# Six shared PSUM banks, attention products of both row halves together, and maxima moved by small DMAs in a gated cross-attention block

## The chip, the cores and the metric

The kernel runs on one core of a Trainium2 chip. The core has a matmul engine (PE, its weight loads are shown as PEld), a vector engine (DVE), a scalar engine for activations (ACT), a general engine (POOL) and a sync engine (SP) that issues DMAs. Each engine works through its own list of instructions in order; semaphores are the only coupling. PE writes to PSUM, which has eight banks of 128 partitions by 512 fp32 numbers, and DVE and ACT read it. The metric is the time of one launch in microseconds (us), the median of some runs.

## What is computed

The reference, cut to what matters (8 batches, 100 queries of width 128, 1444 keys of width 64, 16 heads of width 64, fp32):

```
qh = layernorm(x) @ Wq ; kh = ctx @ Wk ; vh = ctx @ Wv      # split into 16 heads
attn = softmax(qh kh^T / 8)
x = x + tanh(g_xattn) * ((attn @ vh) @ Wo + bo)
z = fp4(layernorm(x))
h = silu(z @ fp4(w_gate)^T) * (z @ fp4(w_up)^T)
x = x + tanh(g_ffn) * (fp4(h) @ fp4(w_down)^T)
```

fp4() rounds blocks of 16 numbers to a grid of 8 magnitudes times a scale of the block.

## The kernel before

Wq is folded with Wk and Wv with Wo ahead of the loop, so that each head scores and sums the raw context of width 64. A **group** is one batch and half of the heads: 8 heads times 100 queries, 800 rows. There are 16 groups (g = 0 to 15), and an even and an odd one make a batch. The 1444 keys are cut into 12 chunks of 120 or 121.

A group has 24 **slots**, one for each chunk c and half k of the 800 rows. In a slot PE makes one tile of scores (keys on partitions, 400 rows as columns) with two matmuls into one bank: L914 (query times key, a split into high and low parts in the 128 partitions) and L915 (the low part of the query, and in seven further rows of `q_ls`, one for each tile of 116 rows, the negated row maximum, so that the bank holds score minus maximum). ACT turns the tile into `probs` (L749, exp). Later L931 multiplies chunks 2j and 2j+1 of one half with the context: two fp32 matmuls into the upper and lower 64 partitions of bank k of `attn`, called a **pair** here. In the profile a pair is four matmul records.

The row maximum is needed before the scores of a group. So while group g runs, PE also makes the scores of group g+1 with rows on partitions (L840, 7 tiles of 116 rows by 3 parts of 482 keys, 21 **maxima**, numbered 0 to 20), DVE reduces each (L1071, `max3`) and then folds them (`max_tiles`, L1112, into `maxes`, one column for each tile). The **shift** use transposes `maxes` with PE into a bank (L843), and DVE spreads it over the seven rows of `q_ls` (L1075).

PSUM is held as two banks of scores (slot modulo 2), two of `attn`, and a ring of four for everything else, handed out in the order of use: the folded query (`q`, L820, read by four ACT copies L638 into `q_hh`, two for each half of the rows, and by two DVE subtractions `split_q`, L1053), the 21 maxima, the shift, the softmax sums (L850), the output products `proj` (L857, read by ACT head by head, L661), and the feed-forward products of the other batches (`xT`, `zT`, `gate`, `up`, `hT`, `down`). A use waits until the use four before it has been read.

The order on every engine is written by hand, by tables of slot numbers: a use that stands at slot s in a table is issued after the scores of slot s, and the pairs of a slot come after its ring uses. `PV_SLOTS` places the 12 pairs (numbers from 24 on fall into the next group), `MAX_SLOTS` the maxima for even and odd groups, `POST_SLOTS` sums and `proj`, `COPY_SLOTS` ACT's copies of `attn`, `CTX_COPY_SLOTS` ACT's six copies that split the next batch's keys, `KLO_AT` the place on POOL of an accumulating DMA that completes those keys (`k_hl`, L600). The first maximum of a group waits for the first two of ACT's four query copies, and in an odd group also for that DMA. Groups 0 and 15 have tables of their own; that of group 15 sets most of its pairs two by two already.

Of the kernel before, what the change touches and what calls it, by code (L numbers as in the profile page):

```python
# [49 lines left out]
SCORE_BANKS, RING_BANKS = 2, 4  # L50
# [20 lines left out]
MAX_SLOTS = [{1: 2, 4: 1, 5: 1, 6: 1, 7: 4, 8: 1, 11: 2, 12: 2, 13: 2, 14: 1, 16: 2, 17: 2}, {1: 1, 3: 2, 6: 1, 7: 4, 8: 1, 9: 1, 10: 2, 13: 1, 14: 2, 15: 4, 17: 1, 18: 1}]  # L71
MAX_TILES_SLOT = [19, 18]
SHIFT_SLOT = [20, 20]
FFN_SLOTS = {1: ('zT', 0), 3: ('gate', 0), 4: ('up', 0)}
DOWN_SLOTS = {4: ('hT', 0), 6: ('hT', 1), 8: ('down', 0)}
LAST_FFN_SLOTS = {**FFN_SLOTS, 20: ('hT', 0), 21: ('hT', 1), 22: ('down', 0)}
W_SLOTS = {(2, 3): ('wT', 0), (2, 14): ('wT', 1), (2, 15): ('wT', 2), (2, 16): ('wT', 3), (2, 19): ('wT', 4), (2, 20): ('wT', 5)}
POST_SLOTS = [{7: ('sum', 0), 8: ('proj', 0), 9: ('proj', 1)}, {6: ('sum', 0), 8: ('proj', 0), 9: ('proj', 1)}]
XT_SLOT = 18
LN2_SLOTS = [13, 14]  # L80
LN2_APPLY_SLOT = 16
Z_SLOTS = [16, 18, 19, 19, 20, 21, 22, 22, 22]
SIGMOID_SLOTS = [4, 5]
H_SLOTS = [18, 19, 20, 21, 22, 22, 23, 23, 23]
# [6 lines left out]
Q_LO_SLOTS = [0, 0]  # L91
HEAD_SLOTS = [7, 7, 8, 9, 9, 9, 9, 9]
LN1_SLOTS = [2, 4, 12]
CTX_COPY_SLOTS = [7, 7, 11, 11, 12, 12]
KLO_AT = 7
# [10 lines left out]
FIRST_MAX_TILES_SLOT, FIRST_SHIFT_SLOT = 20, 21  # L106
# [3 lines left out]
POOL_AT = {'ln1': 2, 'ln2': 6, 'swiglu': (1, 2, 4), 'heads': 5}  # L110


def ring_keys(g, slot):
    keys = []
    pre = g + 1 < GROUPS
    maxima, shift_slot = (MAX_SLOTS[g % 2], SHIFT_SLOT[g % 2]) if g else (FIRST_MAX_SLOTS, FIRST_SHIFT_SLOT)
# [16 lines left out]
    if pre and slot == shift_slot:  # L133
        keys += [("shift", 0)]
# [10 lines left out]
def number_ring():  # L145
    index, n = {}, 0
    for key in START:
        index[(-1, key)] = n
        n += 1
    for g in range(GROUPS):  # L150
        for slot in range(SLOTS):
            for key in ring_keys(g, slot):
                index[(g, key)] = n
                n += 1
    for key in FINISH:
        index[(GROUPS, key)] = n
        n += 1
    return index


RING = number_ring()

# [26 lines left out]
class Turn:  # L189
# [20 lines left out]
    def ring(self, key):  # L210

        i = RING[(self.g, key)]
        return i % RING_BANKS, i // RING_BANKS + 1
# [10 lines left out]
def xattn_ffn(nc, x, ctx_in, g_xattn, g_ffn, Wo, bo, w_gate, w_up, w_down, ctxT_in, WqT, WkT, WvT, out):  # L224
    with ExitStack() as es:
# [7 lines left out]
        scores = es.enter_context(nc.psum_tensor("scores", [128, SCORE_BANKS, 512], F32))  # L233
# [39 lines left out]
        maxes = sb("maxes", [128, TILES])  # L273
# [56 lines left out]
        max_done = sem("max_done")  # L330
        scores_full = sem("scores_full")
# [121 lines left out]
        def _(sp):  # L453
# [36 lines left out]
            def group(t):  # L490
# [15 lines left out]
                if t.g % 2 == 0 and t.g >= 4 or t.g == GROUPS - 1:  # L506
                    store(t)
# [751 lines left out]
```

## Time and profile before

| | |
|---|---|
| median of 3 runs | 548.21 us (547.03 to 548.56) |
| the profiled execution | 547.66 us, of which the span of the trace is 545.8 us |
| PE, PEld busy | 532.4 us (98%), 319.8 us (59%) |
| DVE, ACT, POOL busy | 439.2 us (80%), 312.8 us (57%), 279.9 us (51%) |
| granted PE clock | full speed in all 40 slices |
| DMA | 12.28 MB, most of it in the first slices |

A group of the middle of the kernel takes 31.2 to 31.6 us. "Busy" of PE counts a matmul until its last result has left the array; since matmuls overlap, a busy PE can still have slow places. The chain of work that ended last counts from end to end and shows these.

### The profile page before, as it was taken

The numbers are of one execution on the slowest core, as the hardware profiler recorded it, in microseconds if no ns is written. First come the engines' busy times: TensorE is split into PE (matmuls) and PEld (weight loads), VectorE is DVE, ScalarE is ACT, GpSimd is POOL, SyncE is SP. The second block draws the span as 40 slices with busy tenths as digits, with TensorE's granted clock in tenths as the row PEclk, the third lists the DMA queues.
The fourth block names the chain that finished last, engine by engine and source line by source line (L and its number), as shares of the span: only waits on it lengthen the run. The fifth ranks groups of instructions, "written<-read, shape, count | busy, mean of one in ns | idle before, by whom it ended". The sixth has DMA issues, their size and how long they took to land.

```text
span 545.8 us, 8243 instructions
## 1 busy us (share of the span) xinstructions
PE 532.4 (98%) x2769; PEld 319.8 (59%) x2769; DVE 439.2 (80%) x765; ACT 312.8 (57%) x724; POOL 279.9 (51%) x260
## 2 busy tenths in 40 slices
PE   7989999999999999999999999999999999999997
PEld 4655656656565665656566565756556565655553
DVE  5868889798887979798887978789786988877865
ACT  4365546765467556765467645665567654555611
POOL 4046294745629463574927465383826566184300
PEclk9999999999999999999999999999999999999999
DMA  7502001110012100020011100120000200000000
GB/s 186 114 1 56 0 1 31 29 27 2 1 34 37 19 1 28 9 55 0 2 29 35 28 0 2 36 54 1 1 28 4 29 1 1 5 0 1 2 4 4
DMA packets 10017, 12.28 MB, mean 23 GB/s; under 512 B 4144, under 2 KB 7736, under 8 KB 9976
## 3 DMA queue, kind: packets, MB, share of 16 engines
q1 hardware_dynamic: 9000, 8.85, 6.6%
q0 software_dynamic: 560, 2.59, 3.2%
q8 instruction: 22, 0.36, 0.3%
q10 hardware_dynamic: 416, 0.33, 0.2%
q14 instruction: 19, 0.16, 0.1%
HBM read 11.35 MB, written 0.41 MB: 22 GB/s over the span
## 4 chain that ended last, share of the span: by engine, by line
PE 91%; DVE 6%; issue 2%; ACT 1%; POOL 0%; DVEq 0%; ACTq 0%; POOLq 0%
PE attn L931 28%; PE scores L914 19%; PE ring L840 13%; PE scores L915 12%; PE ring L857 5%; PE ring L850 4%; PE ring L820 3%; DVE max L1071 2%; PE ring L863 2%; PE ring L871 1%; PE ring L843 1%; PE attn L887 1%; ACT q_hh L638 1%; DVE e_gate L1025 0%; PE ring L799 0%
## 5 line engine op out<-in xcount | busy, mean ns | idle before, releaser
L749 ACT ACTIVATE probs<-scores 120x400 f32<-120x400 f32 (+1 forms) x384 | 185.5, 505 | 158.5 <-PE scores L915 156.1
L1071 DVE TENSOR_REDUCE max<-ring 116x1 f32<-116x482 f32 (+2 forms) x336 | 203.5, 651 | 58.2 <-PE ring L840 56.7
L592 POOL TENSOR_TENSOR acc_p<-acc_p,probs 120x800 f32<-120x800 f32 x75 | 145.2, 1936 | 64.2 <-ACT probs L749 59.9
L931 PE MATMUL attn<-probs,ctx_n 120*64 120x400 f32 (+1 forms) x768 | 170.2, 524 | 0.6 <-ACT probs L749 0.6
L914 PE MATMUL scores<-q_hh,k_hl 128*120 128x400 f32 (+1 forms) x384 | 154.6, 402 | 1.2 <-DVE q_ls L1075 0.7
L914 PEld LDWEIGHTS scores<-q_hh,k_hl 128*120 128x120 f32 (+1 forms) x384 | 69.6, 181 | 125.1 <-ACT probs L749 89.5
L915 PE MATMUL scores<-q_ls,k_h 71*120 71x400 f32 (+1 forms) x384 | 133.0, 346 | 0.0
L840 PE MATMUL ring<-k_hl,q_hh 128*116 128x482 f32 (+2 forms) x336 | 111.9, 403 | 1.9 <-DVE q_ls L1053 0.7
L915 PEld LDWEIGHTS scores<-q_ls,k_h 71*120 71x120 f32 (+1 forms) x384 | 70.3, 183 | 3.8
L931 PEld LDWEIGHTS attn<-probs,ctx_n 120*64 120x64 f32 (+1 forms) x768 | 38.3, 134 | 53.6 <-issue 33.5
L840 PEld LDWEIGHTS ring<-k_hl,q_hh 128*116 128x116 f32 (+1 forms) x336 | 58.3, 178 | 12.1 <-DVE max L1071 3.0
L661 ACT ACTIVATE head_out<-ring,rsum 100x128 f32<-100x128 f32 x120 | 37.5, 369 | 30.6 <-PE ring L857 29.0
L1094 DVE TENSOR_TENSOR acc_v<-acc_v,probs 120x800 f32<-120x800 f32 x47 | 47.8, 1017 | 1.7 <-ACT probs L749 1.1
L531 POOL TENSOR_TENSOR stats<-stats,eps 100x1 f32<-100x1 f32 x16 | 3.0, 189 | 88.4 <-DVE stats L1033 88.4
L551 POOL TENSOR_TENSOR head_out<-head_out 100x512 f32<-100x512 f32 (+2 forms) x45 | 43.6, 968 | 6.4 <-ACT head_out L661 4.0
L592 POOL TENSOR_TENSOR acc_p<-probs 121x800 f32<-121x800 f32 x16 | 30.1, 1884 | 30.4 <-ACT probs L749 30.4
L638 ACT ACTIVATE q_hh<-ring 64x400 fp32r<-64x400 f32 x64 | 31.9, 498 | 7.8 <-PE ring L820 6.7
L857 PE MATMUL ring<-vo,attn_sb 128*100 128x128 f32 x256 | 33.3, 273 | 0.0
L857 PEld LDWEIGHTS ring<-vo,attn_sb 128*100 128x100 f32 x256 | 30.7, 166 | 0.9
L442 POOL TENSOR_TENSOR e_gate<-e_gate,ones 100x352 f32<-100x352 f32 x7 | 6.8, 968 | 47.6 <-ACT gate L699 47.6
L850 PEld LDWEIGHTS ring<-ones,acc_v 121*100 121x100 f32 x256 | 25.1, 168 | 1.1 <-issue 0.8
L850 PE MATMUL ring<-ones,acc_v 121*100 121x1 f32 x256 | 24.0, 223 | 0.1
(130 smaller groups left out, 473.4 us busy)
## 6 DMA issues: line engine op xcount, KB each, us to landing
ctx_n<-in_ctx SPq DMA_DIRECT2D x8, 360.0 KB
ctxT<-in_ctxT SPq DMA_DIRECT2D x7, 361.0 KB, 4.0
k_hl<-in_ctxT POOLq DMA_DIRECT2D x7, 361.0 KB, 5.0
wvT<-in_WvT SPq DMA_DIRECT2D x2, 256.0 KB, 4.5
wo<-in_L_xattn_Wo SPq DMA_DIRECT2D x1, 512.0 KB, 5.7
x_in<-in_x SPq DMA_DIRECT2D x8, 50.0 KB
out<-y_out SPq DMA_DIRECT2D x8, 50.0 KB
ctxT<-in_ctxT SPq DMA_DIRECT2D x2, 180.5 KB, 3.9
```

The lines of the kernel that those rows point to most:

```text
L551: pool.tensor_tensor(head_out[0:N, 0:n, :], head_out[0:N, 0:n, :], head_out[0:N, n:2 * n, :], ALU.add).then_inc(head_done, 1)
L592: pool.tensor_tensor(acc_p[0:r, t.g % 2, :], left, probs[0:r, c % PROBS, :], ALU.add).then_inc(sum_p, 1)
L661: op = act.activation(head_out[0:N, h, :], ring[0:N, bank, i * D:(i + 1) * D], ACT.Copy, scale=rsum[0:N, h:h + 1])
L749: act.activation(probs[0:r, c % PROBS, k * HALF:(k + 1) * HALF], scores[0:r, slot % SCORE_BANKS, 0:HALF], ACT.Exp).then_inc(probs_full, 1)
L840: mm = pe.matmul(dst[0:rows, 0:b - a], q_hh[:, (t.g + 1) % 2, tile * TROWS:tile * TROWS + rows], k_hl[par][:, a:b], start=True, stop=True)
L850: mm = pe.matmul(dst[0:N, h:h + 1], acc_v[0:CROWS[0], (t.g + 1) % 2, h * N:(h + 1) * N], ones[0:CROWS[0], 0:1], start=True, stop=True)
L857: mm = pe.matmul(dst[0:N, i * D:(i + 1) * D], attn_sb[:, h * N:(h + 1) * N], vo[:, HG * ((t.g + 1) % 2) + 2 * i + k, :], start=True, stop= ...
L914: pe.matmul(dst, k_hl[par][:, a:a + r], q_hh[:, half, cols], start=True, stop=False)
L915: pe.matmul(dst, k_h1[par][0:C + TILES, a:a + r], q_ls[0:C + TILES, half, cols], start=False, stop=True).then_inc(scores_full, 1)
L931: mm = pe.matmul(attn[64 * i:64 * i + C, k, 0:HALF], ctx_n[0:r, par, c, :], probs[0:r, c % PROBS, k * HALF:(k + 1) * HALF], start=(j == 0) ...
L1071: dve.tensor_reduce(max3[0:rows, tile, part:part + 1], src[0:rows, 0:MAXC[part + 1] - MAXC[part]], AX.X, ALU.max).then_inc(free, 1)
L1094: dve.tensor_tensor(acc_v[0:r, t.g % 2, :], left, probs[0:r, c % PROBS, :], ALU.add).then_inc(sum_v, 1)
```

## The change

- The two score banks and the four ring banks become one ring of six. Scores are uses of the ring like all others, numbered in the order of issue. A use waits for the reader of the use six before it: ACT's exp where that was a score, the old semaphore otherwise.
- `PV_SLOTS` sets the pairs of both halves of a chunk pair into one slot: ten of twelve stand two by two now. Two stay apart, at slots 20 and 21. The last two move from slots 24 and 26 (0 and 2 of the next group) to 25 (1 of the next group).
- The shift use of groups 0 to 14 is gone from PE and DVE. SP issues seven DMAs instead, one for each tile, that copy a column of `maxes` (116 partitions, 4 bytes each) straight into a row of `q_ls` (464 bytes in one partition). The sign moves into the constant rows that multiply them (-1 for 1). The second matmul of slot 0 waits for the first four DMAs, that of slot 1 for all seven. Ahead of the loop the old transposition stays, twice.
- Tables are retuned: maxima (the first of an even group alone in slot 1 now), `COPY_SLOTS` from 2 and 3 to 1 and 4, the second `split_q` from slot 0 to 1, `CTX_COPY_SLOTS` from 7, 7, 11, 11, 12, 12 to 4, 6, 10, 11, 11, 12, `KLO_AT` from 7 to 8, and some links of the feed-forward part by a slot.

```
-SCORE_BANKS, RING_BANKS = 2, 4
+RING_BANKS = 6
...
-PV_SLOTS = [4, 6, 8, 11, 12, 14, 16, 18, 21, 22, 24, 26]
-COPY_SLOTS = [2, 3]
+PV_SLOTS = [5, 5, 9, 9, 13, 13, 17, 17, 20, 21, 25, 25]
+COPY_SLOTS = [1, 4]
...
-KLO_AT = 7
+KLO_AT = 8
...
+            uses += [(g, ("score", slot))] + [(g, key) for key in ring_keys(g, slot)]
...
+            def shift_rows(t):
+                half = (t.g + 1) % 2
...
+                sp.wait_ge(max_done, t.count(1, 3))
+                for tile in range(TILES):
+                    rows = TSIZE[tile]
+                    cols = slice(tile * TROWS, tile * TROWS + rows)
+                    sp.dma_start(q_ls[C + tile:C + tile + 1, half, cols].bitcast(F32), maxes[0:rows, tile:tile + 1].bitcast(F32)).then_inc(shift_in[tile // EARLY_TILES], 16)
...
+            def bank_read(t, key):
+                last = BANK_LAST[(t.g, key)]
...
+                if user[0] == "score":
+                    pe.wait_ge(probs_full, g * SLOTS + user[1] + 1)
+                else:
+                    bank, n = Turn(g).ring(user)
+                    pe.wait_ge(ring_free[bank], n)
...
-                if t.g > 0 or slot >= SCORE_BANKS:
-                    pe.wait_ge(probs_full, t.count(SLOTS, slot + 1 - SCORE_BANKS))
+                bank_read(t, ("score", slot))
...
+                if t.g >= 1 and slot < 2:
+                    for part in range(k + 1):
+                        pe.wait_ge(shift_in[part], shift_count(t, part))
```

**PE, slots 0 to 2 of an even group (8).** The folded query is `ring<-xT,a_all`, a maximum is `ring<-k_hl0,q_hh`, scores are the two rows with 121x400. Before:

```order
L914 MATMUL scores<-q_hh,k_hl0 121x400
L915 MATMUL scores<-q_ls,k_h10 121x400
L820 MATMUL ring<-xT,a_all 128x100 x4
L931 MATMUL attn<-probs,ctx_n 64x400 x2
L914 MATMUL scores<-q_hh,k_hl0 121x400
L915 MATMUL scores<-q_ls,k_h10 121x400
L840 MATMUL ring<-k_hl0,q_hh 116x482 x2
L914 MATMUL scores<-q_hh,k_hl0 121x400
L915 MATMUL scores<-q_ls,k_h10 121x400
L931 MATMUL attn<-probs,ctx_n 64x400 x2
```

After:

```order
L948 MATMUL ring<-q_hh,k_hl0 121x400
L952 MATMUL ring<-q_ls,k_h10 121x400
L854 MATMUL ring<-xT,a_all 128x100 x4
L948 MATMUL ring<-q_hh,k_hl0 121x400
L952 MATMUL ring<-q_ls,k_h10 121x400
L874 MATMUL ring<-k_hl0,q_hh 116x482
L968 MATMUL attn<-probs,ctx_n 64x400 x4
L948 MATMUL ring<-q_hh,k_hl0 121x400
```

The pair that stood between the query and the first maximum stands behind that maximum now, together with the pair of slot 2.

**PE, slots 18 to 23 of the same group**, with the shift (`ring<-ident,maxes`) before:

```order
L931 MATMUL attn<-probs,ctx_n 64x400 x2
L914 MATMUL scores<-q_hh,k_hl0 120x400
L915 MATMUL scores<-q_ls,k_h10 120x400
L914 MATMUL scores<-q_hh,k_hl0 120x400
L915 MATMUL scores<-q_ls,k_h10 120x400
L843 MATMUL ring<-ident,maxes 7x116
L914 MATMUL scores<-q_hh,k_hl0 120x400
L915 MATMUL scores<-q_ls,k_h10 120x400
L931 MATMUL attn<-probs,ctx_n 64x400 x2
```

After, from the two last maxima of slot 17:

```order
L874 MATMUL ring<-k_hl0,q_hh 104x482
L874 MATMUL ring<-k_hl0,q_hh 104x480
L968 MATMUL attn<-probs,ctx_n 64x400 x4
L948 MATMUL ring<-q_hh,k_hl0 120x400
L952 MATMUL ring<-q_ls,k_h10 120x400
L948 MATMUL ring<-q_hh,k_hl0 120x400
L952 MATMUL ring<-q_ls,k_h10 120x400
L948 MATMUL ring<-q_hh,k_hl0 120x400
L952 MATMUL ring<-q_ls,k_h10 120x400
L968 MATMUL attn<-probs,ctx_n 64x400 x2
```

Two pairs stand together behind the last maximum, and the transposition is gone from between the scores.

**SP, an even group and the odd one behind it**, after the change (the seven DMAs close each group):

```order
L466 DMA x_in<-in_x 100x128
L520 DMA ctxT<-in_ctxT 64x1444
L462 DMA ctx_n<-in_ctx_512 120x768
L463 DMA ctx_n<-in_ctx_512 1x256
L495 DMA out<-y_out 100x128
L506 DMA q_ls<-maxes 1x116x1 x6
L506 DMA q_ls<-maxes 1x104x1
L506 DMA q_ls<-maxes 1x116x1 x6
L506 DMA q_ls<-maxes 1x104x1
```

SP's loads and the store of a batch stand ahead of the even group's seven; before, it had nothing in an odd group.

## Rows read from the trace of the kernel before

**Rows 1.** The page: busy time of each engine, and the chain by engine.

```profile
PE 532.4 (98%) x2769; PEld 319.8 (59%) x2769; DVE 439.2 (80%) x765; ACT 312.8 (57%) x724; POOL 279.9 (51%) x260
...
PE 91%; DVE 6%; issue 2%; ACT 1%; POOL 0%; DVEq 0%; ACTq 0%; POOLq 0%
```

**Rows 2.** The chain of waits: start us, length us, work; a stretch of group 5.

```profile
203.26 0.18 PE scores L914
...
203.63 0.82 PE attn L931 x4
204.45 0.37 PE scores L914
...
207.56 0.29 PE ring L843 x2
207.85 0.38 PE scores L914
```

**Rows 3.** The chain in group 15, where pairs already stand two by two.

```profile
506.28 1.49 PE attn L931 x8
507.77 0.38 PE scores L914
...
508.37 0.51 ACT probs L749
```

**Rows 4.** The timeline, start of group 6: start us, us, engine line operation.

```profile
211.01 0.34 PE L914 MATMUL scores<-q_hh,k_hl 128*121 128x400 f32 x1
...
211.37 1.03 PE L820 MATMUL ring<-xT,a_all 128*128 128x100 f32 x8
...
212.44 2.06 ACT L638 ACTIVATE q_hh<-ring 64x400 fp32r<-64x400 f32 x4 [0.34 <-PE ring L820]
...
213.57 0.28 PEld L840 LDWEIGHTS ring<-k_hl,q_hh 128*116 128x116 f32 x2
```

**Rows 5.** The timeline, four maxima of group 5: PE writes, DVE reads.

```profile
202.23 1.03 PE L840 MATMUL ring<-k_hl,q_hh 128*116 128x482 f32 x4
...
202.65 2.36 DVE L1071 TENSOR_REDUCE max<-ring 116x1 f32<-116x482 f32 x4 [0.59 <-PE ring L840]
```

**Rows 6.** The timeline, ACT splits the next batch's keys in group 6.

```profile
229.17 1.51 ACT L649 ACTIVATE k_h<-ctxT 64x722 fp32r<-64x722 f32 x2
...
231.09 1.50 ACT L649 ACTIVATE k_hl<-ctxT 64x722 fp32r<-64x722 f32 x2
```

**Rows 7.** POOL, from 226 us, group 6: its adds and the accumulating DMA.

```profile
228.95 2.63 POOL L551 TENSOR_TENSOR head_out<-head_out 100x512 f32<-100x512 f32 x3
...
235.46 1.90 POOL L592 TENSOR_TENSOR acc_p<-acc_p,probs 120x800 f32<-120x800 f32 x1
...
237.79 0.87 POOL L600 DMA_DIRECT2D k_hl<-in_ctxT  x1 [0.30 <-POOL scratch L598]
```

**Rows 8.** The timeline, PE around the start of group 7, and the maxima fold.

```profile
237.89 0.18 DVE L1112 TENSOR_REDUCE maxes<-max 116x7 f32<-116x21 f32 x1
...
242.39 0.35 PE L914 MATMUL scores<-q_hh,k_hl 128*121 128x400 f32 x1
...
245.10 0.44 PE L840 MATMUL ring<-k_hl,q_hh 128*116 128x482 f32 x1
```

**Rows 9.** Line L600: its DMA from issue to landing.

```profile
DMA to landing us min/median/max: 4.7/5.0/5.2
```

**Rows 10.** SP's issues, spaced, and its wait for the last store (in total, times, longest).

```profile
278.44 0.33 SPq L455 DMA_DIRECT2D ctx_n<-in_ctx  x1
278.81 0.26 SPq L456 DMA_DIRECT2D ctx_n<-in_ctx  x1
...
543.88 0.29 SPq L488 DMA_DIRECT2D out<-y_out  x1
...
SPq L512 <- DMA out<-y_out: 1.2, 1, 1.2
```

**Rows 11.** DMA issues: KB and us from issue to landing, the smallest one.

```profile
tanh_x<-in_g_xattn SPq DMA_DIRECT2D x1, 0.5 KB, 4.3
```

More of the change, by code:

```diff
@@ L145, in number_ring, with count_banks @@
 def number_ring():
[L146 to L149, printed above, removed]
+    uses = [(-1, key) for key in START]
     for g in range(GROUPS):
         for slot in range(SLOTS):
[L152 to L158, printed above, removed]
+            uses += [(g, ("score", slot))] + [(g, key) for key in ring_keys(g, slot)]
+    uses += [(GROUPS, key) for key in FINISH]
+    return {use: n for n, use in enumerate(uses)}
+def count_banks():
+    turn, last, latest = {}, {}, [0] * RING_BANKS
+    users = [None] * RING_BANKS
+    for use, n in RING.items():
+        bank = n % RING_BANKS
+        last[use] = users[bank]
+        latest[bank] += use[1][0] != "score"
+        turn[use] = latest[bank]
+        users[bank] = use
+    return turn, last
 RING = number_ring()
+BANK_TURN, BANK_LAST = count_banks()
 def cell(g, slot):
@@ L330, in xattn_ffn @@
         max_done = sem("max_done")
+        shift_in = [sem(f"shift_in{k}") for k in range(2)]
         scores_full = sem("scores_full")
@@ L505, in group @@
                     load_ctx(t.batch(1), t.parity(1))
-                if t.g % 2 == 0 and t.g >= 4 or t.g == GROUPS - 1:
+                if t.g % 2 == 0 and t.g >= 4:
+                    store(t)
+                if t.g + 1 < GROUPS:
+                    shift_rows(t)
+                else:
                     store(t)
@@ L748, in exps @@
                         act.wait_ge(*added(t, old % CHUNKS, back))
-                act.activation(probs[0:r, c % PROBS, k * HALF:(k + 1) * HALF], scores[0:r, slot % SCORE_BANKS, 0:HALF],
+                act.activation(probs[0:r, c % PROBS, k * HALF:(k + 1) * HALF], ring[0:r, t.ring(("score", slot))[0], 0:HALF],
                                ACT.Exp).then_inc(probs_full, 1)
@@ L841, in ring_use @@
                 elif kind in ("shift", "late"):
-                    pe.wait_ge(max_done, t.count(1, 3) if kind == "shift" and t.g >= 0 else t.count(1, 2))
-                    mm = pe.matmul(dst[C:C + TILES, 0:TROWS], maxes[0:TROWS, :], ident[0:TROWS, 0:TROWS], start=True, stop=True)
+                    pe.wait_ge(max_done, t.count(1, 2))
+                    mm = pe.matmul(dst[C:C + TILES, 0:TROWS], maxes[0:TROWS, :].bitcast(F32), ident[0:TROWS, 0:TROWS], start=True, stop=True)
                 elif kind == "sum":
@@ L901, in score_slot @@
                 par, half, r, a = t.parity(), t.g % 2, CROWS[c], COFF[c]
[L902 to L903 removed]
+                bank_read(t, ("score", slot))
                 if slot == 0:
[L905 removed]
+                    wait_reads(pe, (t.before(), ("q", 0)))
                     if t.g == 0:
+                        wait_reads(pe, (t.before(), ("shift", 0)))
                         pe.wait_ge(consts_set, 9)
```

72 lines of the change are left out of this document (38 added, 34 removed).

## The prediction, made before the changed kernel was run

> **What bounds the kernel now.** I read the page first: PE is busy 98% of the span, and 91% of the chain that ended last is PE's [rows 1]. So the time is PE's list of work, and what other engines do costs only where PE waits for them. In the middle of the kernel it never does: a scores matmul takes its 0.18 us in the chain again and again. The next question is where this full engine is slow. The chain shows it: a pair of attention products takes 0.82 us, and the first scores matmul behind it 0.37 us where 0.18 is plain [rows 2]. Two pairs in a row take 1.49 us, less than twice 0.82, and the penalty of the next scores comes once [rows 3]. So entering and leaving the attention products costs PE time although it counts as busy. By the busy share alone only the idle rest, 545.8 - 532.4 = 13.4 us, could be won; by the chain more can.
>
> The Trainium skill (Trainium Kernel Development and Optimization, section Performance Expectations) calls matmul busy time a bad metric because matmuls are pipelined. If busy time were a good metric, 547.66 - 13.4 = 534.3 us would be the floor of this change; the trace agrees with the page, since its chain shows busy stretches that take longer than others for the same products.
>
> The sum is made against the profiled execution, 547.66 us, which lies 0.55 us under the median.
>
> **Pairs two by two (a gain).** Two lone pairs with the scores behind them: 2 x 0.82 + 2 x 0.37 = 2.38 us [rows 2]. Together: 1.49 + 0.38, and one plain 0.18: 2.05 us [rows 3]. Each merge gives 0.33 us. Groups 1 to 14 have 12 clusters of pairs before and 7 after, so 14 x 5 = 70 merges: **-23.1 us**. All of it is on PE's path.
>
> **The shift leaves PE (a gain).** The transposition takes 0.29 us and makes the next scores matmul 0.38 instead of 0.18 [rows 2]: 0.49 us, 15 times: **-7.4 us**. DVE loses its spreading operation too; DVE is not on the path there.
>
> **Six banks in group 15 (a gain).** Twice in its double pairs' neighbourhood PE waits there for an exp of 0.51 us because scores have two banks [rows 3]; with six it need not: **-1.0 us**.
>
> Gains: 31.5 us, which alone would make 516.2.
>
> **The first maximum of a group (a cost).** It needs two of ACT's four copies of the folded query. Before, these were just covered: the query's matmuls end at 211.37 + 1.03 = 212.40, the copies start at 212.44, four take 2.06, so two are done at 213.47, and the maximum's weight load starts at 213.57 [rows 4]. Nothing is to spare. Between query and maximum PE had a pair with its penalty (0.82 + 0.19) and one slot of scores (0.37). The change moves the pair behind the maximum; PE arrives 1.0 us earlier and must stand still, and everything behind it in its list, the double pair and the scores, stands too. In an even group the wait is 1.0 us; in an odd one `zT` and 0.1 us of slack (245.10 - 242.39 = 2.7 us after the start, not 2.6 [rows 8]) leave 0.9. For groups 1 to 14: 7 x 1.0 + 7 x 0.9 = **+13.3 us**. The copies cannot start before the query ends, so this has one answer.
>
> **Scores behind maxima in one ring (a cost).** PE writes a maximum each 0.22 us, DVE reads one each 2.36 / 4 = 0.59 us [rows 5]. Before, a score never waited for DVE. Now it does, if the use six before it was a maximum. The dense place is slots 14 to 17: in an odd group 8 maxima and 4 slots of scores, 8 x 0.22 + 4 x 0.37 = 3.2 us for PE and 4.7 us for DVE. By hand, counting reads from the first write: the scores of slot 17 need the fourth read and come 0.2 to 0.3 us early; an even group loses 0.1 at `xT` and 0.2 at the last maximum. Bounds: nothing, and one read, 0.59 us, in each of 14 groups (8.3). I take 0.3: **+4 us**.
>
> **ACT behind in even groups (a cost).** The key copies stood in pairs of 1.5 us [rows 6]; now they are spread, one before and two behind the exp of slot 10 and 11, on top of the head scalings. By hand the exp of slot 11 ends 0.3 us after PE wants its bank for slot 13. Bounds: nothing, and one copy, 0.75 us, in 7 groups (5.3). I take **+2 us**.
>
> **The accumulating DMA (a cost).** It is issued 237.79 - 211.01 = 26.8 us after an even group's start, behind the heads' sum of 2.63 us and its adds of 1.90 us [rows 4, 7]. POOL's chain begins with the exp that ACT does between head scalings, and those follow `proj`, which comes no earlier now, since PE lost at the first maximum what it had won. With `KLO_AT` = 8 one more add of 1.9 stands ahead: 28.5 us or so; it lands 5.0 us later [rows 9], at 33.5. The group then lasts about 31.2 - 1.6 - 0.5 + 1.0 + 0.6 = 30.7 us, so the landing is 2.8 us into the next one, where the maximum is ready at 2.6: 0.3 to 0.4 us more. Groups 5 to 13, five times: **+2 us**. Bounds: nothing, and a whole add five times (9.5).
>
> **The seven DMAs (a cost, or none).** Before, 242.39 - 238.07 = 4.3 us lay between the fold's end and the next group [rows 8]. Now a double pair stands behind the last maximum, but the shift and one more lone pair are gone from that stretch. PE's work from the last maximum to the second matmul of slot 0 is 1.49 + 0.56 + 0.37 + 0.37 + 0.82 + 0.56 + 0.82 + 0.56 + 0.37 + 0.19 = 6.1 us, in an odd group 0.37 more; DVE's reads and the fold lag the last maximum by 1.9 (even) or 2.8 (odd). That leaves 4.2 and 3.7 us. The fourth DMA is issued 3 x 0.37 + 0.1 = 1.2 us after the fold, by the spacing of 278.44 and 278.81, and a store of 100 rows lands 0.29 + 1.2 = 1.5 us from its issue [rows 10]: 2.7 us, covered. The seventh lands at 3.8 us, and slot 1 wants it 1.2 us later than slot 0 wants its four. The upper bound is the only DMA of 4-byte pieces in the trace, 4.3 us to landing, though it queued behind the weights [rows 11]: 1.2 + 4.3 = 5.5, a wait of 1.3 and 1.8 us, 15 times 23 us. I take the store's price, since the queue is as empty here as there, and **+1 us** for group 1, whose fold is late. The cover is the lone pairs of slots 20 and 21, 2 x 1.0 us; without them the DMAs would be bare.
>
> **Sum.** 547.66 - 31.5 + 13.3 + 4 + 2 + 2 + 1 = **538.5 us**. With all uncertain costs at nothing it is 529.5; with those of ring, ACT and POOL at twice their values 546.5.
>
> **Rival 1, the gain stays whole at the first maximum.** If the copies came earlier or the order of arrival were other than the list says, 9 to 13 us of waits would not appear: 547.66 - 31.5 + 9 = 525. Against it: in-order lists, and the weight load 0.1 us behind the second copy. Chance 0.06.
>
> **Rival 2, the shared ring costs twice as much.** DVE is busy 80% [rows 1], and with a shorter group 85%; if it comes to slot 14 with a backlog, each dense stretch waits for more than one read. 546.5 us. For it: many places where a score now hangs on DVE. Against it: after the wait at the first maximum each group starts relaxed. Chance 0.17.
>
> **Rival 3, slower: the DMAs land late.** Mechanism: 116 pieces of 4 bytes written into one partition are nothing like the store's rows of 512 bytes; PE waits between the two matmuls of slot 0, and the whole list behind it. Price: with 4.3 us to landing 1.3 to 1.8 us in each of 15 groups, 538.5 + 23 = 562. It decides from a wait of 9.2 / 15 = 0.6 us a group on, which is a fourth landing 4.6 us behind the fold, a DMA of 3.4 us. Chance 0.12.
>
> The Trainium skill (DMA: Bandwidth & Descriptors, section Why a DMA increments its semaphore by 16 and not by 1) states that such a copy runs on the largest number of engines up to 16 that divides its slowest dimension; 116 gives four, so four DMAs would queue 116 pieces on each of the same four engines. By that rule rival 3 needs some (3.4 - 1.5) / 116 = 0.02 us a piece to come true, an estimate. No row here has the time of such a piece, so the chance above stays.
>
> **Chances.** The forecast 0.65, the rivals 0.06, 0.17 and 0.12. The range of 530 to 547 holds the forecast with its unknown costs and rival 2, and leaves out rivals 1 and 3. This kernel's measurement can tell 0.3% from no change, 1.6 us. Faster by more than that is the forecast, rival 1 and two thirds of rival 2, 0.83; within it 0.05; slower 0.12.
>
> **What the profile of after would show.** The chain with `attn` x8 of 1.49 and some 117 clusters instead of 187; no transposition inside groups. ACT's `q_hh` as the releaser of the first maximum's matmul or weight load, about 1 us in each group, 13 us in all; that would be the largest wait. DVE's maxima as releaser of scores or maxima at slots 15 to 17, under 0.6 us each. In odd groups the accumulating DMA as the last wait of slot 1. No wait for `q_ls` DMAs, or a few tenths; if they show over 0.6 us a group, rival 3 holds. A group should last 30.4 to 30.8 us. The prediction is wrong if the first maximum starts without a wait, or if scores wait for DVE in many slots.

## The result: slower, 578.4 us

| | before | after |
|---|---|---|
| median of the runs | 548.21 us | 578.38 us (569.75 to 581.87, 4 runs) |
| the profiled execution | 547.66 us | 569.75 us |
| its span, granted clock | 545.8 us, 1.000 | 567.9 us, 0.967 |
| PE busy | 532.4 us (98%) | 527.1 us (93%) |

Two of the four executions after count as slow; the ratio of the times without them is 1.045, 95% interval 1.039 to 1.052. The forecast was 538.5 us, faster; rival 3, late DMAs, had 562. The page of the kernel after, first the busy times [rows 1], then PE's busy tenths and its granted clock in 40 slices:

```profile
PE 527.1 (93%) x2739; PEld 334.4 (59%) x2739; DVE 429.8 (76%) x750; ACT 311.1 (55%) x724; POOL 275.2 (48%) x261
...
PE   7889998989999799979999799997999899998997
PEclk9889999979999899998999899997999989999999
```

PE is busy 5.3 us less, as the merges want it, but it stands 40.8 us of the span where it stood 13.4. And the clock row, whole for the kernel before, has a notch every fourth or fifth slice: one in each odd group from group 3 on. (The one in the second and third slice, around the start of group 0 and inside it, is another; it is there with the shift on PE too.) The waits (engine and line, what it waited for, us in total, times, longest) name the cause:

```profile
PE ring L952 <- DMA q_ls<-maxes: 23.9, 15, 2.9
```

L952 is the second matmul of a tile of scores, the one that reads the seven rows of maxima. That is the place that rival 3 named. The timeline shows one case, the end of group 6 and the start of group 7 (start us, us, engine line operation; in brackets the idle time ahead of it and what ended it):

```profile
246.02 0.17 DVE L1151 TENSOR_REDUCE maxes<-max 116x7 fp32r<-116x21 f32 x1
...
246.22 5.55 SPq L506 DMA_DIRECT2D q_ls<-maxes  x7
...
247.89 0.88 POOL L623 DMA_DIRECT2D k_hl<-in_ctxT  x1 [0.29 <-POOL scratch L621]
...
250.31 0.35 PE L948 MATMUL ring<-q_hh,k_hl 128*121 128x400 f32 x1
...
253.53 0.45 PE L952 MATMUL ring<-q_ls,k_h 71*121 71x400 f32 x1 [2.87 <-DMA q_ls<-maxes]
253.82 1.31 PE L854 MATMUL ring<-xT,a_all 128*128 128x100 f32 x8
```

The maxima are folded at 246.19, 4.12 us ahead of the group (250.31), as in [rows 8] and as the budget of the forecast had it. Four DMAs should be done 2.7 us later. PE can go on only 7.3 us later. Between them and their landing lies line L623: the accumulating DMA of 361 KB, in the same stretch. The windows around it (length us, then busy time of PE, PEld, DVE, ACT, POOL, the granted clock, the share of the 16 DMA engines, GB/s) show what it does:

```profile
247.50:249.40 1.90, 1.90 (x10) 0.48 (x6) 1.82 (x3) 0.95 (x3) 1.60 (x3) 1.00 0.14 9
249.40:252.20 2.80, 1.26 (x7) 0.84 (x5) 2.73 (x5) 0.90 (x2) 1.30 (x1) 1.00 0.90 132
252.20:253.50 1.30, 0.00 (x0) 0.00 (x0) 1.27 (x3) 0.00 (x0) 0.00 (x0) 1.00 0.15 1
```

The packets of the trace go with that. Each small DMA shows as 120 packets of 4 bytes and 9 ns. Three DMAs, 360 packets, pass from 247.54 to 249.09. From 249.44 to 252.19 run the 64 packets of 5776 bytes of the accumulating DMA, at 90% of the engines. The small ones begin again at 251.5, and 451 of their 477 start after 252.0. So the fourth DMA stands behind the large transfer for some 3 us, and lands 7.3 us behind the fold, in groups 5 to 13 always 7.1 to 7.3 us. (The trace doesn't tell which of the 16 engines a packet went through; that they are what is shared is read from their busy share of 0.90.)

The second cost follows. PE has stood 2.9 us, and then the clock falls to its lower level (1.2 GHz): the eight matmuls of the folded query take 1.31 us where they took 1.03 [rows 4]. The windows after that:

```profile
254.40:261.20 6.80, 6.51 (x21) 3.52 (x20) 3.69 (x5) 3.60 (x9) 0.00 (x0) 0.50 0.00 0
261.20:268.00 6.80, 6.80 (x42) 4.79 (x42) 4.66 (x6) 4.13 (x10) 4.45 (x4) 1.00 0.00 0
```

At half clock 21 matmul records fit in 6.8 us, at full clock 42. The odd groups with a stretch of 3.4 us at half clock (5, 9, 13) last 35.1 us, groups 7 and 11 with 6.8 us 36.3; group 3, which stood only 1.6 us, also has 6.8 us of it and lasts 35.0. Even groups from 4 to 12 last 30.8 to 31.0. The profiled execution of the kernel before had no such stretch in its loop. The four executions took 569.75, 577.45, 579.3 and 581.87 us at mean clocks of 0.967, 0.950, 0.947 and 0.941.

**A balance.** I took from the trace the start of each PE instruction, and summed how much later each came behind its forerunner than the same two kinds mostly do. This excess is 61.8 us in the kernel after and 8.0 in the one before. 547.66 - 31.5 (the gains of the forecast) + 53.8 = 569.96; measured 569.75. That it closes to 0.2 us is luck: the sum hangs on what is taken as the usual distance, and other choices on the same traces give 44 to 50 us for 53.8, so gains of 22 to 28 us. One merge can be read directly. From the start of the scores matmul ahead of a pair to that of the third one behind it are 1.565 us with a lone pair, 2.236 with a double pair and 0.555 with none: 2 x 1.565 - 2.236 - 0.555 = 0.34 us, where the forecast had 0.33. So the merges came as forecast, and most of the error lies among the costs.

### The profile page after: what moved, and what is told of

Read it like the earlier page. It is cut to its first block and busy times, and to the rows that moved or that the text cites. A ratio compares the mean times of both kernels' runs of the same rounds, so it can differ in the third digit from the quotient of the medians.

```text
span 567.9 us, 8289 instructions
## 1 busy us (share of the span) xinstructions
PE 527.1 (93%) x2739; PEld 334.4 (59%) x2739; DVE 429.8 (76%) x750; ACT 311.1 (55%) x724; POOL 275.2 (48%) x261
## 5 line engine op out<-in xcount | busy, mean ns | idle before, releaser
L772 ACT ACTIVATE probs<-ring 120x400 f32<-120x400 f32 (+1 forms) x384 | 184.7, 504 | 165.2 <-PE ring L952 162.1
L1107 DVE TENSOR_REDUCE max<-ring 116x1 f32<-116x482 f32 (+2 forms) x336 | 200.7, 649 | 75.5 <-PE ring L874 73.3
L968 PE MATMUL attn<-probs,ctx_n 120*64 120x400 f32 (+1 forms) x768 | 163.3, 539 | 1.4 <-ACT probs L772 1.4
L952 PE MATMUL ring<-q_ls,k_h 71*120 71x400 f32 (+1 forms) x384 | 136.6, 356 | 23.9 <-DMA q_ls<-maxes 23.9
L948 PE MATMUL ring<-q_hh,k_hl 128*120 128x400 f32 (+1 forms) x384 | 153.5, 400 | 1.6 <-DVE q_ls L1111 0.7
L948 PEld LDWEIGHTS ring<-q_hh,k_hl 128*120 128x120 f32 (+1 forms) x384 | 71.4, 186 | 87.9 <-issue 64.8
L952 PEld LDWEIGHTS ring<-q_ls,k_h 71*120 71x120 f32 (+1 forms) x384 | 71.8, 187 | 34.2 <-DMA q_ls<-maxes 20.1
L968 PEld LDWEIGHTS attn<-probs,ctx_n 120*64 120x64 f32 (+1 forms) x768 | 46.3, 141 | 64.8 <-issue 46.2
L573 POOL TENSOR_TENSOR head_out<-head_out 100x512 f32<-100x512 f32 (+2 forms) x45 | 39.8, 884 | 6.2 <-ACT head_out L684 3.8
L661 ACT ACTIVATE q_hh<-ring 64x400 fp32r<-64x400 f32 x64 | 31.9, 499 | 8.2 <-PE ring L854 7.0
L1089 DVE TENSOR_TENSOR q_ls<-ring,q_hh 64x400 fp32r<-64x400 f32 x32 | 18.2, 570 | 21.0 <-ACT q_hh L661 20.5
L891 PEld LDWEIGHTS ring<-vo,attn_sb 128*100 128x100 f32 x256 | 31.2, 166 | 0.4
```

The lines of the kernel that those rows point to most:

```text
L573: pool.tensor_tensor(head_out[0:N, 0:n, :], head_out[0:N, 0:n, :], head_out[0:N, n:2 * n, :], ALU.add).then_inc(head_done, 1)
L772: act.activation(probs[0:r, c % PROBS, k * HALF:(k + 1) * HALF], ring[0:r, t.ring(("score", slot))[0], 0:HALF], ACT.Exp).then_inc(probs_fu ...
L891: mm = pe.matmul(dst[0:N, i * D:(i + 1) * D], attn_sb[:, h * N:(h + 1) * N], vo[:, HG * ((t.g + 1) % 2) + 2 * i + k, :], start=True, stop= ...
L948: pe.matmul(dst, k_hl[par][:, a:a + r], q_hh[:, half, cols], start=True, stop=False)
L952: pe.matmul(dst, k_h1[par][0:C + TILES, a:a + r], q_ls[0:C + TILES, half, cols], start=False, stop=True).then_inc(scores_full, 1)
L968: mm = pe.matmul(attn[64 * i:64 * i + C, k, 0:HALF], ctx_n[0:r, par, c, :], probs[0:r, c % PROBS, k * HALF:(k + 1) * HALF], start=(j == 0) ...
```

## Experiments

All are changes of the kernel after unless said otherwise; all were timed beside the kernel before, 548.1 us in each comparison.

### Is it the DMAs, the collision, or the clock?

**The shift on PE again.** The ring, the merged pairs and the tables stay; maxima go through PE's transposition and DVE's spreading, as before.

```
+SHIFT_SLOT = [20, 20]
+    if pre and slot == shift_slot:
+        keys += [("shift", 0)]
...
-                if t.g + 1 < GROUPS:
-                    shift_rows(t)
```

> The changed kernel with one part undone: the row maxima go through PE's transposition and DVE's spreading again (slot 20), no small DMAs; ring of six, double pairs and all tables stay. Theory D (the loss is the wait for the small DMAs at the start of odd groups, plus the half clock that follows it): the DMA waits of 23.9 us and the half-clock stretches inside the loop vanish, the transposition costs 7.4 us of PE again, the wait of 1 us at each first maximum and about 0.4 to 0.7 us a group behind DVE and ACT stay: 545 us, 541 to 549, and all executions within 1%. Rival R (the six-bank ring and the double pairs themselves cost what was lost): still over 560 us with the waits for DVE and ACT as large as ever.

Measured 543.63 us (543.08 to 544.31), ratio 0.989 (0.985 to 0.994). Its page:

```profile
PEclk9889999999999999999999999999999999999999
```

No notch behind group 0. Without the DMAs the change is 4.5 us faster than before, with them 30.2 slower: they cost 34.7 us by the medians (25.4 by the profiled executions), though they spare PE 7.4. Its waits show the term of the forecast at the first maximum, in even groups for ACT's copies, in odd ones for `z_fp`, which the product `zT` just ahead of the maximum needs:

```profile
PE ring L862 <- ACT q_hh L649: 6.9, 10, 0.8
PE ring L882 <- DVE z_fp L439: 5.6, 7, 1.2
```

**The large DMA made small.** The accumulating DMA carries 2 KB instead of 361; the low part of the keys is left out by that, everything else stays.

```
-                pool.dma_start(k_hl[b % 2][0:C, :], ctxT_in[b, :, :], accum_op=ALU.add)
+                pool.dma_start(k_hl[b % 2][0:1, 0:512], ctxT_in[b, 0:1, 0:512], accum_op=ALU.add)
```

> The changed kernel, but POOL's accumulating DMA moves 2 KB (one row of 512 numbers) instead of 361 KB. It leaves out most of the low part of the keys from batch 1 on. Theory C (the seven small DMAs are held up behind the accumulating DMA's packets, which share their DMA engines): the waits of 3 us at the start of groups 3, 5, 7, 9, 11, 13 vanish, and with them the half-clock stretches of these groups; the wait of 2 us at group 1, where the fold comes late, stays: 542 us, 538 to 547. Rival P (116 pieces of 4 bytes are slow by themselves): the waits at odd groups stay near 3 us and the time near 570.

Measured 544.15 us, ratio 0.990 (0.985 to 0.995). Its waits:

```profile
PE ring L952 <- DMA q_ls<-maxes: 12.3, 15, 1.9
```

The small DMAs are all still there. In the same place as above the second matmul of slot 0 now starts 0.18 us behind the first, not 3.2. The 12.3 us left are 1.9 in slot 0 of group 1, where the fold comes late, and for the rest in slot 1, for the seventh DMA, which lands together with the query copies the first maximum wants anyway. Odd groups from 5 on last 30.8 us instead of 35.1 to 36.3. POOL still issues its DMA at the same place, 1.65 us behind the fold. So what costs 34 us isn't the size or number of the small DMAs, nor the issue of the other one, but the 361 KB that run beside them.

With nothing beside them the fourth small DMA lands 4.0 us behind the fold and the seventh 6.0, where the forecast had 2.7 and 3.8. PE wants the fourth 4.1 us behind the fold in even groups and 4.3 in most odd ones: it is covered with 0.1 to 0.3 us to spare, and the seventh isn't covered.

**The wait filled.** In odd groups three matmuls whose result nobody reads stand ahead of the wait in slot 0.

```
+                if t.g % 2 and t.g + 1 < GROUPS and slot == 0:
+                    bank_read(t, ("q", 0))
+                    keep_warm(3, ring[:, t.ring(("q", 0))[0], :])
```

> The changed kernel with three throwaway matmuls of 128x512 (0.85 us each) between the two scores matmuls of slot 0 in odd groups 1 to 13, that is inside the wait for the small DMAs; they write the bank that the folded query overwrites. Theory K (half of the loss is the clock that falls because PE stands still there): the wait stays, filled, the granted clock stays at full speed in the loop, and the time is 560 us, 556 to 564, with all executions close together. If the clock falls for another reason: no gain, 570 us or more, and the spread of 12 us between executions stays.

Measured 557.84 us, ratio 1.016 (1.011 to 1.021); its start of group 7, and its clock:

```profile
246.96 0.35 PE L948 MATMUL ring<-q_hh,k_hl 128*121 128x400 f32 x1
247.15 2.75 PE L921 MATMUL ring<-ones,ident 128*128 128x512 f32 x6
249.99 0.44 PE L955 MATMUL ring<-q_ls,k_h 71*121 71x400 f32 x1
250.26 1.03 PE L854 MATMUL ring<-xT,a_all 128*128 128x100 f32 x8
...
PEclk9899999999999999999999999999999999998999
```

The second matmul still starts 3.0 us late, but the query takes 1.03 us, and the clock holds in these groups. 2.75 us of useless work in each of seven groups makes the kernel 20.5 us faster by the medians, 11.4 by the profiled executions. So of the 34 us about 20 were the clock (about 11 against the profiled execution), and 12 to 14 the wait itself: the odd groups from 3 on last 33.1 to 33.6 us here, 30.6 to 30.8 without the collision. Group by group, a stretch of 3.4 us at half clock made a group 1.5 to 1.9 us longer, one of 6.8 us 2.8 to 2.9 (1.9 in group 3). If PE's work simply took twice as long, it would be 1.7 and 3.4: little of it is hidden.

**The large DMA moved.** DVE takes POOL's add of chunk 4 and POOL that of chunk 9. I wanted POOL to come to the accumulating DMA 1.9 us sooner by that.

```
-SUM_V = [0, 3, 9, 10, 11]
+SUM_V = [0, 3, 4, 10, 11]
```

> The changed kernel, small DMAs and all, with the exchange of chunks 4 and 9 between DVE and POOL. POOL then has one add less ahead of the accumulating DMA, which starts 1.9 us earlier, some 4.5 us before the group's end instead of 2.5, just before the fold's small DMAs. Theory C (the small DMAs wait until the big one's packets are through): they are still held up, but it is through 1.9 us earlier, so the wait at odd groups falls from 3.0 to 1 to 1.5 us, the clock falls less often, and the time is 540 to 556 us with the DMA waits near 12 us in all. If the collision did not depend on when the big DMA runs: 3.0 us as before and 570.

```profile
PE ring L952 <- DMA q_ls<-maxes: 20.2, 15, 2.6
```

570.16 us, ratio 1.040, where 540 to 556 was expected. The edit didn't do what I wanted. POOL now stands 5.8 us for ACT's first `head_out` (in group 6), and behind that it has the same three adds ahead of the DMA as in the kernel after; it issues it 0.3 us later than in the kernel after, here 1.99 us behind the fold (251.08) instead of 1.70:

```profile
253.07 0.87 POOL L623 DMA_DIRECT2D k_hl<-in_ctxT  x1 [0.29 <-POOL scratch L621]
```

Its packets begin 3.5 us behind the fold instead of 3.2, and in that gap those of the fourth small DMA pass: mostly 480 packets ahead of the large ones, not 360. So the wait leaves slot 0 in the odd groups from 5 on (second matmul 0.19 us behind the first in most) and comes back in slot 1, 1.8 to 2.6 us long, since now the fifth to seventh DMA meet the large one, and each of these groups has its 3.4 us of half clock. A shift of 0.3 us decides which small DMAs are held up; that fits the collision. The total says nothing on an earlier large DMA, which stays untried, and it holds the harm of the exchange itself, 17 to 23.5 us in other kernels (below).

### Which part of the rest pays?

**Pairs merged in the kernel before**, with its two score banks and ring of four:

```
-PV_SLOTS = [4, 6, 8, 11, 12, 14, 16, 18, 21, 22, 24, 26]
+PV_SLOTS = [5, 5, 9, 9, 13, 13, 17, 17, 20, 21, 24, 24]
```

> The kernel before with one table changed: its pairs stand two by two, in slots 5, 9, 13, 17, 20, 21 and 24 (PV_SLOTS 5,5,9,9,13,13,17,17,20,21,24,24); two score banks, ring of four, transposition on PE and all other tables as before. Measures the merges alone. If each merge gives 0.33 us and nothing new waits: 547.7 - 23.1 = 524.6. Theory B (six shared banks are needed for double pairs, because four ring banks and two score banks run dry around them): waits for DVE and ACT eat 10 us or more, over 534.

555.91 us, ratio 1.014 (1.011 to 1.018). Five merges should take 1.65 us from a group, but the groups last 32.1 to 32.3, not 31.2 to 31.55. So new waits take 32.3 - 31.2 + 1.65 = 2.75 us from an even group and 32.1 - 31.55 + 1.65 = 2.2 from an odd one. The largest are two for DVE in odd groups: the first scores wait 0.5 us for the spreading of the shift (L1075), and a feed-forward product (`up`) 0.5 us for the read of a maximum. The rest are scores that wait for ACT and maxima that wait for DVE. Before and here:

```profile
PEld ring L840 <- DVE max L1071: 3.0, 8, 0.5
```

```profile
PEld ring L840 <- DVE max L1071: 11.8, 31, 0.9
```

With two score banks and the tables of before the merges don't pay. What retuned tables would give there was not run.

**The ring of six in the kernel before**, with its tables:

> The kernel before with the ring of six for scores and all other products and nothing else: its tables, lone pairs and the transposition on PE as before. Theory H (a score behind a maximum waits for DVE): 1 to 6 us slower than before in waits at dense slots, less the 1 us that group 15 gains: 547 to 553. Rival (six banks in common are never worse): 546 to 547.

555.67 us, ratio 1.015 (1.011 to 1.018), more than expected. Its groups last 31.8 and 31.95 (maxima and scores wait for DVE's reads, 0.5 to 0.6 us a group), and groups 0, 2 and 6 are longer than before by 1.4, 1.6 and 1.6 us. The trace shows part of where: in group 0 the transposition waits 0.75 us for the fold; in groups 2 and 6 PE waits 0.3 and 0.4 us for DVE's subtraction of the query, and at a maximum 0.8 and 0.9 us for DVE's reads, 0.3 in the other even groups. Why DVE is late just there stays open. The ring costs alone and the merges cost alone; together, with the retuned tables, they are the 543.6 us of the first experiment. How much of that is the tables no run tells.

### What holds the start of a group?

543.6 is 4.5 us better than before, although the merges bring 23. The groups from 4 to 13 last 31.05 and 31.2 us, before 31.2 and 31.55; and group 0 lasts 35.9 us for 32.8. The forecast has most of the reason: +13.3 at the first maximum. I tried to win that back on the kernel with the shift on PE.

**The first maximum a slot later**, to slot 2, so that ACT has time to copy:

> As e1 (transposition on PE), and the first maximum of each group moves from slot 1 to slot 2, behind the double pair, so that the double pair covers ACT's two query copies. Theory Q (the first maximum's wait for the copies is a loss of 1 us in each of 14 groups): 14 us less than e1, near 531 us, 527 to 536, and no wait between the query and the double pair. Rival: the wait is absorbed by a later one (DVE reads in the dense slots), then no more than 5 us less than e1.

```profile
220.12 0.60 PE L862 MATMUL ring<-k_hl,q_hh 128*116 128x482 f32 x2
...
221.73 0.39 PE L889 MATMUL ring<-ident,h_fp 100*128 100x100 f32 x2 [0.65 <-DVE q_ls L1073]
...
223.65 0.48 PE L862 MATMUL ring<-k_hl,q_hh 128*116 128x480 f32 x1 [0.78 <-DVE max L1091]
```

558.39 us, ratio 1.016, where 531 was expected; wrong by 27. The wait for the copies is gone, and two for DVE stand in its place: `hT` needs the bank from which DVE subtracts the query, and the next maxima need DVE's reads. Even groups last 31.9, odd ones 31.5. The clock takes part in the loss: groups 2, 12 and 14 are 3.5, 2.5 and 2.3 us longer than in the first experiment, each with a stretch of half clock.

**The last double pair a slot earlier** (24), and then also both subtractions in slot 0:

> As e1 (transposition on PE), and the last double pair of a group moves from slot 25 to slot 24, that is directly behind the folded query of the next group, ahead of scores slot 1; the maxima stay where they are. Theory Q (the double pair can cover the query copies and zT): the 1.0 us waits at zT or the first maximum vanish in all groups, 14 us less than e1, 530 us. Theory V (what stands behind the wait is DVE, which at a group's start works off its backlog in order, as e4 hints): only odd groups gain their full 1 us, even ones wait for the query's bank and for the first maxima's reads instead: 534 to 538 us.

> As e5, and DVE's second subtraction of the query moves back from slot 1 to slot 0, ahead of the add of the last chunk, so that the query's bank comes free 1 us earlier and the first maximum's read some 0.2 us earlier. Theory V: the wait of hT for the query's bank in even groups shrinks by up to 0.9 us, 0 to 5 us less than e5. Theory Q: no change against e5, since nothing waits there.

544.30 (0.993) and 543.87 us (0.992). The groups last 31.05 and 31.23 us in the first, within 0.05 us those of the first experiment, and 31.15 and 31.02 in the second. The waits have moved, all to DVE: in the first `hT` (0.7 us) and `gate` (1.0) wait for its subtractions, in the second scores wait 0.9 and 0.4 us for its reads of maxima. So at a group's start ACT and DVE are both late by the same 1 us, and DVE has no gap there.

**An add taken from DVE.** The exchange of chunks 4 and 9 on the three kernels with the shift on PE:

> As e1 (transposition on PE, double pair in slot 25), and the sums of probs are shared out otherwise: DVE adds chunk 4 (slot 11) instead of chunk 9 (slot 21), and POOL takes 9 instead of 4; the number of adds on each engine stays. Theory V (DVE works without a gap from a group's last maxima to the next group's first, and PE waits for it there): 0.98 us less in that stretch. In e1 the first maximum of an even group waits for ACT's copies anyway, so only odd groups (zT) gain: 4 to 8 us less than e1, 536 to 540. Theory Q (only ACT's copies bound): no change, 544.

> As e5 (double pair in slot 24, so ACT's copies are covered) with the same exchange of chunks 4 and 9. Theory V: e5 gained nothing on e1 because DVE's backlog took the place of the copies; with 1 us less of it per group this should be the place where both show: 10 to 14 us less than e5, 530 to 534. Theory Q, or a bound elsewhere (dense maxima): under 4 us less than e5.

> As e10, with DVE's second query subtraction in slot 0 ahead of the last add. Theory V: the query's bank comes free 1 us earlier, which frees hT and gate; 0 to 3 us less than e10.

567.13, 563.84 and 560.52 us (1.033, 1.029, 1.023): 17 to 23.5 us slower than without the exchange, instead of 4 to 14 faster. (A link is one of the DVE operations in a row that make `z_fp` of `z`.) DVE at the same place, first with the shift on PE alone, then with the exchange, and POOL beside the latter:

```profile
240.41 2.07 DVE L429 TENSOR_TENSOR f_abs<-z,f_small 100x128 f32<-100x128 f32 x1
242.52 0.23 DVE L431 TENSOR_SCALAR f_t<-f_abs 100x128 int32<-100x128 int32 x1
```

```profile
248.55 2.08 DVE L429 TENSOR_TENSOR f_abs<-z,f_small 100x128 f32<-100x128 f32 x1
250.67 1.92 DVE L431 TENSOR_SCALAR f_t<-f_abs 100x128 int32<-100x128 int32 x1
```

```profile
248.29 4.22 POOL L603 TENSOR_TENSOR acc_p<-acc_p,probs 120x800 f32<-120x800 f32 x2
```

L431 takes 0.23 us, or 1.92 beside POOL's second add. A DVE link that meets an add of POOL ends just behind it (252.59 and 252.51 here). The exchange took 0.98 us from DVE and put 1.7 on it, and the product `zT` waits 2.1 us for `z_fp` in most odd groups (14.1 us in all) instead of 0.8 (5.6 in all); the clock then falls in the loop as in the kernel after. The Trainium skill (SBUF — State Buffer, section SBUF: two separate sides) has the rule: VectorE and GpSimd share one pair of ports by an exclusive lock, and a DVE operation with two SBUF inputs, or in a mode that uses both ports, and a GpSimd operation that reads SBUF exclude each other for the length of the instruction. The rows agree for L429, which has two inputs (2.07 us for 0.29). L431 has one; that it runs in such a mode no row shows.

**An add given to DVE**, to test that the other way: `SUM_V` = [0, 3, 7, 9, 10, 11] and [0, 3, 8, 9, 10, 11] with the shift on PE, the first also with the pair in slot 24 and both subtractions in slot 0.

> The kernel of e1_pe_shift (543.6 us) with one of the seven adds of the softmax sums per group, that of chunk 7, taken from POOL (1.9 us there) and given to DVE (1.0 us there); the mirror of e9_add_to_pool, which gave DVE's add of chunk 9 to POOL and became 23 us slower. Theory L (blocking): a DVE operation with two SBUF inputs stands still while POOL adds. In e1 the link f_abs<-z,f_small lasts 2.07 us beside POOL's last add where the same shape lasts 0.29 alone; in e9 two links stood, 2.08 and 1.92 us. With one add less POOL is done before DVE's links: the link shows 0.3 us, z_fp in odd groups comes at least 1 us earlier and PE's wait for it (1.0 us, 7 groups) goes: odd groups 30.2 to 30.7 us, even ones 31.0 to 32.0, total 536 to 546. Theory M (DVE's load alone): one more add on DVE makes every group start of DVE 1 us later; the link stays at 2.07, PE's waits grow by 1 us in both kinds of group: 558 or more.

> As e13_add_7_on_dve, but with chunk 8's add on DVE in place of chunk 7's. Theory L: the same relief for the links, but DVE's extra add comes two slots later, beside the last maxima, where DVE is dense: up to 1 us later fold in each group. 538 to 550. Theory M: 558 or more, link still 2.07.

> The kernel of e6_pairs_24_q_low (543.9 us; last double pair in slot 24, both query subtractions in slot 0) with chunk 7's add on DVE. Theory L: the relief of e13, and since the double pair no longer stands behind the first maximum, less of it is taken back by the next wait: 533 to 544. Theory M: 558 or more.

551.9 (1.007, interval 1.004 to 1.009), 547.57 (0.999) and 549.32 us (1.002). Line L429 (its shortest, median and longest time in ns) in the first two:

```profile
L429 DVE TENSOR_TENSOR f_abs<-z,f_small x8: 292/1394/1415, 119.0 to 534.3; 100x128 f32<-100x128 f32 x8
```

```profile
L429 DVE TENSOR_TENSOR f_abs<-z,f_small x8: 292/293/293, 120.0 to 534.7; 100x128 f32<-100x128 f32 x8
```

The kernels are slower by 4 to 8 us than those without the exchange, neither 5 faster nor 14 slower. With chunk 8's add gone from POOL the link lasts 0.29 us in all groups, and `zT` in group 7 comes 0.16 us late instead of 1.0. So the blocking is shown, and DVE's load alone, under which the link would stay at 2.07, falls. Yet nothing is won. The same place in that kernel:

```profile
250.30 0.28 PE L882 MATMUL ring<-ident,z_fp 100*128 100x100 f32 x1
251.26 0.44 PE L862 MATMUL ring<-k_hl,q_hh 128*116 128x482 f32 x1 [0.68 <-ACT q_hh L649]
```

The row names ACT, but the copies end 2.46 us into the group, and in odd groups the maximum also needs the accumulating DMA. In groups 5, 7, 9, 11 and 13 that one lands 3.30, 2.46, 2.78, 3.22 and 2.85 us into the group, and the maximum starts 0.25 us behind it each time (3.55, 2.71, 3.03, 3.46, 3.10). The list of waits puts only one of these down to it:

```profile
PE ring L862 <- DMA k_hl<-in_ctxT: 1.4, 1, 1.4
```

POOL issues it 29.2 us into the even group here, 28.3 with the shift on PE alone, where it lands 1.9 to 2.2 us into the odd one, ahead of the copies. So with the link out of the way the next owner is the term "The accumulating DMA" of the forecast. Even groups last 31.2, most odd ones 30.9 to 31.8 us, against 31.05 and 31.2 without the added work. (The profiled execution took 552.2 us, the longest of ten.) With chunk 7 the DMA lands 1.2 to 1.5 us in and the copies are the bound, but the extra add stands ahead of the fold, and the transposition waits 0.8 us for it.

## Why the prediction was wrong

**The step that failed is "The seven DMAs".** It priced a small DMA by a store "since the queue is as empty here as there", 2.7 us to the fourth, and took +1 us. The queue was empty; the engines behind it weren't, and the fourth landed 7.1 to 7.3 us behind the fold in groups 5 to 13. With the clock that fell behind that wait it cost 34 us, not 1. The page of the kernel after has the large one's time as in [rows 9] (KB, us to landing):

```profile
k_hl<-in_ctxT POOLq DMA_DIRECT2D x7, 361.0 KB, 5.0
```

The term above it in the forecast had this transfer's time, issued 28.5 us into an even group and 5.0 us long. It was issued 247.89 - 219.33 = 28.56 us into group 6 and took those 5.0. The two terms were never laid side by side: the small DMAs are issued from 26.9 us on, and the large one's packets run from 30.1 to 32.9. I asked of the large DMA only when it lands and not what it stands in the way of. Row for row the evidence was there [rows 7 to 9]. The upper bound, 1.8 us a group, was taken from a DMA near nothing, and rival 3 looked for the cause in the size of the pieces. It had the place right and the cause wrong, so that it named a slower kernel is in part luck: the pieces take 9 ns, half the 0.02 us an even split over four engines would have needed; such a DMA lands 2.0 us behind its issue where nothing runs beside it, not 3.4; and at the end of odd groups, where no large DMA runs, the fourth lands in time.

The spacing was mis-sized too: SP starts one of these every 0.64 us, not every 0.37 (line L506; the numbers are the shortest, median and longest issue in ns), so the fourth is issued 2.0 us behind the fold instead of 1.2, and lands another 2.0 later instead of 1.5. Without the collision these 4.0 us were just covered, as the small accumulating DMA showed; the 6.0 of the seventh were not, and slot 1 waits 0.5 to 1.0 us for it in most groups, also in even ones.

```profile
L506 SPq DMA_DIRECT2D q_ls<-maxes x105: 597/598/1500, 53.3 to 515.8; - x105
```

**There was no term for the clock.** [Rows 1] and the clock row of before gave no hint, since PE never stood for 3 us there. A rival with a wait of 1.3 to 1.8 us in each group should have asked what the clock does after it; here it cost 11 to 20 us beside the 12 to 14 of the wait. Rival 3's price of 562 was short of the result for that reason, 578.

**The other terms.** Most held in size. The measured waits are counted as in the balance, as time by which a start came late.

| term | forecast | measured |
|---|---|---|
| group without the DMAs' harm | 30.4 to 30.8 us | 30.8 to 31.0 |
| gains | 31.5 us | 31.5 by my count, 22 to 28 by others; 0.34 us a merge for 0.33 |
| wait ahead of the first maximum | 1.0 us | 1.04 (group 8) |
| ACT behind at slot 13, even groups | 0.3 us | 0.32 |
| scores behind maxima | 0.3 us a group | 0.40 (group 8), 0.45 (group 9) |
| accumulating DMA lands in an odd group | at 2.8 us, +2 us in all | at 2.3 to 2.7 us, behind a longer wait; 1.9 to 2.2 and no wait with the shift on PE |
| shift off PE, in the end | 7.4 us won | nothing |

The last line wants a word. PE is spared 15 × 0.49 us, and waits for the DMAs in slot 1 instead. The kernel with the transposition, 543.63, and that with DMAs but no collision, 544.15, are the same within their spreads. I read from that, and from the experiments on a group's start, that PE isn't the bound there, so that what leaves PE is given back as a wait; no run shows it by itself.

The wait ahead of the first maximum has one flaw in its reading. The forecast named ACT's copies as the releaser; in the kernel after, PE stands in slot 1 for the seventh DMA, which lands at the same time, and comes to the maximum just as the copies are done:

```profile
220.76 2.07 ACT L661 ACTIVATE q_hh<-ring 64x400 fp32r<-64x400 f32 x4 [0.31 <-PE ring L854]
...
222.01 0.41 PE L952 MATMUL ring<-q_ls,k_h 71*121 71x400 f32 x1 [1.08 <-DMA q_ls<-maxes]
222.26 0.38 PE L874 MATMUL ring<-k_hl,q_hh 128*116 128x482 f32 x1
```

Size and place right, releaser another; the even groups of the kernel with the shift on PE show the copies bare, 0.8 us of idle time each.

**The faster kernel.** The ring and the merged pairs with the shift left on PE, 543.63 us (0.989, 0.985 to 0.994), beats both; that with the last double pair in slot 24 (543.87) is the same.

**Open.** How the extra time splits between wait and clock in the executions of 577 to 582 us of the kernel after is known only by their mean clocks. The ring's 1.4 to 1.6 us in groups 0, 2 and 6 of the kernel before have a place but no cause. Why group 3, after 1.6 us of standing, had 6.8 us at half clock, and group 1, after 1.85, none, no run tells. And a large DMA issued well ahead of the fold, the plain remedy, was not run.

## What to carry over

Before a latency-critical DMA is added, lay all transfers of that stretch on one time axis, those of other engines' queues too: an empty queue doesn't mean an empty engine behind it. Price a wait of PE with the half clock that can follow it, and ask of each gain on a full engine whether that engine is the one that is late at that very place; here 1 us a group had three owners (ACT's copies, DVE's operations, the landing of the large DMA), and removing one showed the next. Where an operation waits for several things, compare the end of each with its start: the one that the profile names need not be the last. POOL work beside short DVE operations isn't free: an add moved to POOL held DVE longer than it had cost there.

## What the runs showed of the hardware

- A DMA of 116 single numbers from 116 partitions into one row ran as 120 packets of 9 ns; SP issued one every 0.64 us, and it landed 2.0 us behind its issue. Beside it 64 packets of 5776 bytes held its next packets up for about 3 us.
- After PE had stood 2.7 to 2.9 us, the granted clock was at its lower level for 3.4 or 6.8 us; after 1.6 us it fell once (group 3), after 1.85 once not (group 1); with 2.75 us of filler in the wait it stayed whole.
- DVE operations of 0.23 and 0.29 us from SBUF to SBUF lasted 1.9 and 2.1 us beside an add of POOL; reads of a maximum from PSUM lasted 0.66 us at most beside one, as without it.
